# Second attention of a Flamingo-style block: the next batch's tokens turned by the DMA crossbar instead of TensorE, and their parts made by GpSimd

## What is computed

```python
def _L1_xattn_ref(x, latents, gamma_media, beta_media, gamma_lat, beta_lat, Wq, bq, Wkv, bkv, Wo, bo):
    xn = _layernorm(x, gamma_media, beta_media)
    ln = _layernorm(latents, gamma_lat, beta_lat)
    q = ln @ Wq + bq
    kv_input = jnp.concatenate([xn, ln], axis=1)
    kv = kv_input @ Wkv + bkv
    ...
    q = q * DH ** (-0.5)
    sim = jnp.einsum('bhid,bhjd->bhij', q, k)
    attn = jax.nn.softmax(sim, axis=-1)
    out = jnp.einsum('bhij,bhjd->bhid', attn, v)
    return out @ Wo + bo
```

## Time and profile before

| what | value |
|---|---|
| median of 3 runs | 801.98 us (799.04 to 802.85) |
| the profiled execution's own time | 799.78 us |
| its span, first to last instruction | 798.0 us |
| mean granted TensorE clock | 0.98 |
| busy TensorE / VectorE / ScalarE / GpSimd | 742.0 / 675.6 / 515.0 / 267.3 us |
| one batch of the second attention (499.08 to 557.40 us) | 58.32 us, of it TensorE 57.65, VectorE 52.79, ScalarE 39.87, GpSimd 20.70 |

### The profile page before, as it was taken

The page is one execution under the profiler, slowest core; times in us unless marked ns, Lnnn a source line. Parts: engine busy times, 40 slices in busy tenths (PEclk is TensorE's granted clock), DMA queues, the critical chain, the costliest instruction groups (busy, mean ns, idle before and its releaser), DMA issues. The chain is left out here.

```text
span 798.0 us, 14791 instructions
## 1 busy us (share of the span) xinstructions
PE 742.0 (93%) x4888; PEld 595.5 (75%) x4888; DVE 675.6 (85%) x1643; ACT 515.0 (65%) x1103; POOL 267.3 (33%) x375
## 2 busy tenths in 40 slices
PE   5799999998998999999999999999999999995896
PEld 4577777766656787888888888898888888884333
DVE  5778888788887999998998999998988987985697
ACT  4266666676763666666666766676676677664665
POOL 3433333331022133333332332343333323342645
PEclk9699999999999999999999999999999999998899
DMA  4934443320501454445435344444444443452003
GB/s 122 145 124 130 129 130 123 116 88 3 171 1 33 103 93 93 103 104 93 67 69 91 68 78 81 74 82 101 78 85 83 75 72 69 77 97 56 0 1 106
DMA packets 180619, 68.12 MB, mean 85 GB/s; under 512 B 152688, under 2 KB 178864, under 8 KB 180544
## 3 DMA queue, kind: packets, MB, share of 16 engines
q1 hardware_dynamic: 178048, 66.32, 38.9%
q0 software_dynamic: 2496, 0.87, 0.8%
HBM read 17.46 MB, written 2.10 MB: 25 GB/s over the span
## 5 line engine op out<-in xcount | busy, mean ns | idle before, releaser
L1889 ACT ACTIVATE c_pS<-c_pS,c_neg_max 128x512 f32<-128x512 f32 x126 | 83.5, 663 | 122.1 <-DVE c_neg_max L2079 122.1
L1815 POOL CAST c_pT<-c_turned 128x1024 fp32r<-128x1024 f16 x84 | 88.1, 1049 | 176.6 <-PE c_pO L2430 110.9
L2079 DVE TENSOR_REDUCE c_neg_max<-c_pS 128x1 f32<-128x512 f32 x126 | 86.1, 684 | 24.8 <-PE c_pS L2415 24.7
L571 DVE TENSOR_REDUCE a_neg_max<-ab_ps 128x2 f32<-128x512 f32 x128 | 82.4, 684 | 27.4 <-PE ab_ps L818 26.4
L2063 DVE SCALAR_TENSOR_TENSOR c_planes<-c_pS,c_r_sum,c_planes 128x512 f16<-128x512 f32 x126 | 93.4, 741 | 1.5 <-ACT c_planes L1896 1.5
L2430 PE MATMUL c_pO<-c_pT,c_v_hi 128*128 128x256 f32 x504 | 94.2, 284 | 0.0
L410 ACT ACTIVATE a_probsT<-ab_ps 128x512 f32<-128x512 f32 x128 | 69.4, 595 | 29.7 <-PE ab_ps L831 29.2
L1896 ACT ACTIVATE c_planes<-c_pS,c_r_sum 128x512 f16<-128x512 f32 x126 | 86.1, 683 | 1.8 <-DVE c_r_sum L2087 1.7
L2430 PEld LDWEIGHTS c_pO<-c_pT,c_v_hi 128*128 128x128 f32 x504 | 82.6, 190 | 5.5 <-POOL c_pT L1815 0.2
L2399 PE MATMUL c_pV<-w_hi,c_kv 128*128 128x512 f32 x248 | 78.1, 396 | 5.2 <-DVE c_kv L2043 5.2
L2371 PE MATMUL c_pK<-c_kv,w_hi 128*128 128x512 f32 x252 | 78.7, 393 | 1.3 <-PEq L1650 1.3
(11 more groups left out here) (432 smaller groups left out, 1928.4 us busy)
## 6 DMA issues: line engine op xcount, KB each, us to landing
a_q_stack<-w_hi SPq DMA_DIRECT2D x94, 64.0 KB, 2.6
a_k_stack<-w_hi SPq DMA_DIRECT2D x48, 64.0 KB, 2.7
c_kv<-w_hi SPq DMA_DIRECT2D x42, 64.0 KB, 2.6
s_ctx<-in_ctx_dram SPq DMA_DIRECT2D x8, 256.0 KB, 4.0
x_sb<-in_x_dram SPq DMA_DIRECT2D x8, 256.0 KB, 4.5
ctx_in<-in_ctx_dram SPq DMA_DIRECT2D x8, 256.0 KB, 2.9
out_dram<-x_sb SPq DMA_DIRECT2D x7, 256.0 KB, 2.2
c_turned<-c_planes SPq DMA_TRANSPOSE x86, 3.0
```

Of the source, the lines that this page charges most:

```text
L571: nc.vector.tensor_reduce(neg_max[:, r // 2 % 2, e, r % 2, :], pS[:, e, :, :], AX_X, ALU.max, negate=True).then_inc(s["max"], 1)
L1815: nc.gpsimd.tensor_copy(pT[:, :, :, half], turned[n % 3].rearrange("p (a t) q -> p a t q", a=2)).then_inc(s["cast"], 1)
L1889: nc.scalar.activation(unit_bank(n), unit_bank(n), ACT.Exp, bias=neg_max[:, u % 4:u % 4 + 1], accum_out=sums[:, u % 4:u % 4 + 1]).then_inc ...
L2079: nc.vector.tensor_reduce(neg_max[:, u % 4:u % 4 + 1], unit_bank(n), AX_X, ALU.max, negate=True).then_inc(s["max"], 1)
```

## The change

1. The norms of batch b+2 are begun in batch b (slots 8 to 15), half a batch sooner than before; the context is loaded sooner; `ctx_normed` writes in place. Own tokens are normed into the second half of `kvn`, which later holds the turned tokens (`kvf`). `out_normed`, `out_stats` and `bias_in` move to slots 6, 3 and 2, and the feed-forward weights' scaling and casts to other batches.
2. `turn_kv` is gone. GpSimd splits the normed tokens into two fp16 planes (`token_planes`, a cast and a subtraction, for context and own tokens each), SyncE sends them through the crossbar (`turn_tokens`), GpSimd adds the two turned planes (`token_sum`). The norms are scaled by 2^10 and gamma by 2^-10, so that the low plane keeps its digits.
3. `kv_affine` now works in place in SBUF, in slots 4 and 6 (6 and 9 in the first batch), after `exps` and ahead of `k_high`.
4. `kv_parts` is GpSimd's instead of VectorE's.

```diff
+            def turn_tokens(i):
+
+                sp.wait_ge(s["zp"], i + 1)
+                wait(sp, s["zsum"], i)
+                sp.dma_start_transpose(z_turned.rearrange("p (a q) -> p a q", q=P), z_planes).then_inc(s["z"], DMA)
...
+                    if u == (5 if b == 0 else 2) and b + 1 < B:
+                        turn_tokens(2 * b)
+                    if u == (8 if b == 0 else 5) and b + 1 < B:
+                        turn_tokens(2 * b + 1)
...
-                    if u == 11 and b + 2 < B:
+                    if u == (6 if b == 0 else 2) and b + 2 < B:
                         ctx_batch(b + 2)
...
+            def token_planes(i):
+
+                m, half = i // 2 + 1, i % 2
+                pool.wait_ge(s["latn" if half else "ctxn"], m)
+                wait(pool, s["z"], DMA * i)
+                source = kvn[:, TT:KT, :] if half else ctx_in[:, :, :]
+                nc.gpsimd.tensor_copy(z_parts[:, :, 0, :], source).then_inc(s["zhi"], 1)
+                pool.wait_ge(s["zhi"], i + 1)
+                nc.gpsimd.tensor_tensor(z_parts[:, :, 1, :], source, z_parts[:, :, 0, :], ALU.subtract).then_inc(s["zp"], 1)
+
+            def token_sum(i):
+
+                pool.wait_ge(s["z"], DMA * (i + 1))
+                pool.wait_ge(s["zp"], i + 1 if i % 2 else i + 2)
+                wait(pool, s["kv_lo"], i)
...
+            def kv_parts(i):
+
+                m, half = i // 2 + 1, i % 2
+                high, low = (kv[m % 2][:, y, :, half * T:(half + 1) * T] for y in range(2))
+                pool.wait_ge(s["kvf"], i + 1)
+                nc.gpsimd.tensor_copy(high, kvf).then_inc(s["kv_hi"], 1)
+                pool.wait_ge(s["kv_hi"], i + 1)
+                nc.gpsimd.tensor_tensor(low, kvf, high.bitcast(F32), ALU.subtract).then_inc(s["kv_lo"], 1)
...
+                    elif not last:
+                        if i == 0:
+                            token_planes(2 * b + 1)
+                        if i == 1:
+                            token_sum(2 * b)
+                        if i == 2:
+                            kv_parts(2 * b)
+                            token_sum(2 * b + 1)
+                        if i == 3:
+                            kv_parts(2 * b + 1)
...
+                    if i == 7 and b + 2 < B:
+                        token_planes(2 * (b + 1))
...
-                    if u in (6, 8) and not last:
-                        kv_affine(b + 1, u // 2 - 3)
                     high(n + 2, u + 2)
                     exps(n + 3, u + 3)
+                    if u in ((6, 9) if first else (4, 6)) and not last:
+                        kv_affine(2 * b + (u > (6 if first else 4)))
...
-                    if u in (6, 8) and not last:
-                        kv_parts(b + 1, 1 - par, u // 2 - 3)
...
                 if j == 0:
-                    wait(pe, s["kv_lo"], DC * n)
+                    wait(pe, s["kv_lo"], 2 * n - 1)
+                if j == TT:
+                    wait(pe, s["kv_lo"], 2 * n)
...
-                        if u in (5, 7) and not last:
-                            turn_kv(b + 1, u // 2 - 2)
```

More of the change, by code:

```diff
@@ L66 @@
 UP = 2.0 ** 14
+Z_UP = 2.0 ** 10
 FF = 704
@@ L1860, in _, with kv_affine @@
         def _(act):
[L1861 to L1867 removed]
+            def kv_affine(i):
+                side = i % 2
+                act.wait_ge(s["zsum"], i + 1)
+                act.wait_ge(s["gamma"], 1)
+                for c in range(DC):
+                    last = nc.scalar.activation(kvf[:, c, :], kvf[:, c, :], ACT.Identity, bias=beta[:, side, c:c + 1], scale=gamma[:, side, c:c + 1])
                 last.then_inc(s["kvf"], 1)
@@ L2227, in others @@
                     if u == 6:
+                        out_normed(b - 1)
+                    if u == (8 if last else 9):
+                        out_size(b - 1)
+                    if u == 2 and not last:
                         bias_in(b)
[L2229 to L2237 removed]
+                if u == 0 and b in (1, 2, 4, 5):
+                    ffn_whole(b // 4, range(FT // 2) if b in (1, 4) else range(FT // 2, FT))
+                if u == 0 and b == 3:
+                    ffn_row_scales(1)
+                if first and u == 6:
+                    bias_in(0)
+                if last and u == 0:
+                    down_scales()
+                if last and u == 2:
+                    down_whole()
+                if last and u == 7:
+                    bias_in(b)
+                if b + 2 < B:
+                    if u == 8:
+                        own_stats(b + 2)
                     if u == 10:
[L2239 removed]
+                        ctx_stats(b + 2)
+                    if u == 11:
+                        aggregate(b + 2, stats, moments, var_eps, "", KT)
                     if u == 12:
[L2241 removed]
+                        own_normed(b + 2)
                     if u == 13:
[L2243 to L2251 removed]
+                        lat_stats(b + 2)
+                        aggregate(b + 2, stats_l, moments_l, var_eps_l, "_l", TT)
+                    if u == 14:
+                        ctx_normed(b + 2)
+                    if u == 15:
+                        lat_normed(b + 2)
             def tail():
@@ L2344, in _ @@
             W = (w_hi, w_lo)
-            def turn_kv(n, c, bank=pQ):
-                pe.wait_ge(s["latn"], n)
-                if not isinstance(n, int) or n > 0:
-                    pe.wait_ge(s["q_lo"], H1 * (n - 1) + (6, 7)[c])
-                for t in range(KT):
-                    last = nc.tensor.transpose(bank[:, t * P:(t + 1) * P], kvn[:, t, c * P:(c + 1) * P], ident[:, :])
-                last.then_inc(s["kv"], 1)
             def turn_x3(m, bank=pQ):
```

129 lines of the change are left out of this document (50 added, 79 removed).

## The result

The changed kernel takes 807.99 us (median of 10 runs, 804.38 to 810.25) against 802.04 for the kernel before (10 runs, 799.04 to 804.97) on the same chip: 1.0069 times as long, with a 95% interval of 1.0054 to 1.0084. It is slower, by about 6 us, where 801.3 and no clear difference were forecast. The profiled execution took 810.25 us, its span 808.5; it is the slowest of its ten, while that of the kernel before (799.78) lies 2.3 under its median.

What follows compares the result with a forecast made beforehand. TensorE was taken to set the pace; -1.8 us (batches 1 to 6), +1.4 (batch 0) and -0.3 (row scales) made -0.7 on the median 801.98, so 801.3 us. Range 791.5 to 808.0; the forecast's own, 797 to 807.

Steps and rivals of the forecast that it cites:

- What bounds the kernel: Second attention: TensorE, busy 57.65 of 58.32 us a batch, sets the pace; a plain slot takes 3.50.
- What is removed: Two turn_kv a batch (0.98 us) and slot 9's wait for kv_parts (0.89): 1.87 a batch, 11.2 for batches 1 to 6.
- The chain on GpSimd and SyncE: Crossbar transfers, planes, casts and sums finish early in batches 1 to 6; head 1's casts have 1.3 us to spare.
- Rival C: Turned planes land late, delaying head 1's casts or token_sum: 807.9 us, near 813 at 2.1 late; C and D together 0.20.
- Where it comes back: Slots 2 to 8: waits for k_lo and GpSimd's port lock make VectorE late; TensorE pays 1.57 us a batch.
- The forecast's signs: Among others, in slot 8 of batches 1 to 6 TensorE waits over 1 us for c_oT_lo before the output product.
- the ledger: VectorE's work and waits against TensorE's 7.00 us per two slots: late by 0.60, 0.77, then 2.23 in slot 8.
- The affine pair's term: Slots 4 and 6: ScalarE's pair before k_high brings k_lo 3.07 us after the maximum; VectorE waits 0.96 in each.
- Rival A: Slot 6: out_normed gets in before GpSimd's subtraction, 1.0 us less lateness in slot 8; 795.3 us, chance 0.20.
- The tolerance: In an even slot VectorE may be 0.66 us late; TensorE pays all lateness beyond that.
- Batch 0: VectorE is already slower; slot 8's wait grows about 1.5 us, slot 10's keys come 2.3 late: net 1.4 slower, bounds 0 and 3.
- B (absorbed): VectorE's lateness in slot 8 stays within 0.66 us, so all 1.87 a batch is kept: 791.9 us, chance 0.17.

Runs made afterwards that it cites:

- the version with three moves: The changed kernel with the affine pair ahead of the exponentials, bias_in in slot 12 and the output norm in its old slots: 789.19 us, 0.9849 of the kernel before.

## Why the prediction was wrong

**What bounds the kernel: right.** TensorE set the pace, and where nothing kept it waiting the six batches came to 56.4 to 57.1 us.

**What is removed: right.** Slot 9 takes 3.53 instead of 4.42, and the eight transposes are worth 6.2 us measured by themselves.

**The chain on GpSimd and SyncE: right in batches 3 to 5**, where the planes' cast began 3.3 us after the issue and the casts of head 1 ended 0.7 to 1.5 us before `values` (forecast 1.3). In batches 1 and 2 they ended 0.3 and 0.4 before it. It was wrong in batch 6. Rival C was given a chance for two transposes in a row; the planes came late only in the batch that has the weights' transposes too. That these are the cause is likely, not shown: spread over two batches they left the planes at 5.45 us.

**Where it comes back: right in kind, short in size.** This is the step that failed: "So a batch gains 1.87 - 1.57 = 0.30; six give 1.8." TensorE's standstill rose, and batches 1 to 6 lost 3.6 us, 5.7 away from the forecast (-1.8, and -0.3 for the row scales). The forecast's signs came: TensorE waited 0.96 to 1.12 us for `c_oT_lo` in slot 8 of each of these batches. But in batch 4 it paid 0.15 + 0.79 + 1.29 = 2.23 us in slots 4, 6 and 8, not 1.57, and that is 58.81 less the 56.58 of the version with three moves. By terms of the ledger:

- The affine pair's term was right: `k_lo` came 3.08 us after the maximum in slots 4 and 6 (529.40 to 532.48, 537.23 to 540.31), forecast 3.07. The profile calls 1.09 us of it a wait; 0.12 of that is a gap which stands there without the pair too.
- `bias_in` lost 1.1, not 0.8: 0.3 more; in batches 5 and 6, at 2.41 and 2.65 us for the pair, 1.6 and 1.8. The bounds (0.5 to 1.7) nearly held.
- The variance was entered with its 0.36 us, as if it were too small to be hit. It was blocked for 0.4 to 0.8 us in each batch. This term was missing altogether, and it is the largest of the misses, 0.7 us in batch 4. What the forecast applied to the wide norm happened to an operation on 2 numbers a partition as well: it waited for the rest of GpSimd's instruction.
- The output norm lost 0.86 in batch 4, not 1.0. Rival A's margin of 0.24 was enough (540.98 less 540.81, so 0.17).
- The tolerance was right. In each of the 16 even slots of batches 1 to 6 that were lengthened by VectorE, its lateness less what TensorE paid over 3.50 is 0.65 to 0.67 us (forecast 0.66). In slots 4, 6 and 8 of batch 4 VectorE's maximum came 1.70, 2.35 and 2.84 us after TensorE's start (at 529.40, 537.23 and 545.50), so 0.80, 1.45 and 1.94 us late with the 0.9 of the forecast. The forecast had 0.60, 0.77 and 2.23, and payment in slot 8, or some in slot 6.

Together the corrected terms make 0.9 us more (0.3 + 0.7 - 0.1); measured were 0.7 more in batch 4. The rest lies in the 5.35 us of plain work for two slots, which measured 0.1 to 0.2 less. Batches 5 and 6 missed by most, by 1.6 and 1.5 us: batch 5 with 2.41 us for `bias_in` behind the scaling of the weights (1.47 us in slot 1), batch 6 with the planes' wait.

**Batch 0: right in kind, short in size.** +4.84 instead of +1.4. Slot 8 grew by 1.73 (forecast 1.5), slot 9 gave back 1.50 (1.47). Slot 10 grew by 3.78, where 2.3 was forecast: the wait was 2.1, and the fall of the clock behind it added 1.4. That this fall came here, and not behind slot 8 or nowhere, is a matter of the single execution. Slot 14 grew by 0.95; no term stood for it. A norm of batch 2 now stands just ahead of it, but no run tries batch 0 without it.

**The rivals.** B (absorbed) had the right floor, 56.5 us a batch, for a version that keeps VectorE out of GpSimd's way. C had its mechanism in one batch. The case that came true was none of them: the forecast's own mechanism with larger terms, and its own range ended at 807. That the wide range reached 808.0, where the measured time lies, is owed to C's late planes and so is luck. A gain of 0.30 that is the difference of 1.87 and 1.57 should have had both signs beside it with nearly equal chances.

**What stays open.** How the 1.0 and 0.8 us that batches 3 and 5 take over batch 4 divide between GpSimd's casts of the weights and VectorE's scaling of them, which was not tried; why the planes are slower in batches 2 and 6; and what decides whether the clock falls behind a wait of over 2 us.
